# Attention with triangular systems: the diagonal blocks move by copies and 32x32 transposes instead of through DRAM

## The chip, the cores and the metric

The kernel runs on one core of a Trainium2 chip, as one program. The metric is the device time of an execution in microseconds; of several executions the median counts. TensorE is called PE in the profile, VectorE DVE, ScalarE ACT, GpSimd POOL, and SyncE SP; a DMA queue belongs to the engine that issues its transfers (SPq, ACTq).

## The reference, cut to what matters

The program is a transformer of two layers on 2 x 512 tokens of width 256. Each layer is a residual of an attention and of a mixture of experts, each behind a layer norm. The change touches only the attention of layer 0, which has 16 heads of width 16:

```python
s = einsum("bihd,bjhd->bhij", k, k) * scale      # keys with keys, strictly below the diagonal
p = exp(s - max) / sum                           # softmax over j < i
A = p * beta[..., None] + eye(T)                 # unit lower triangular, T = 512
u = solve_triangular(A, v, lower=True)
o = softmax(q k^T * scale, causal) @ u
```

So for each batch and head a triangular system of 512 x 512 is solved, with one right-hand side of 16 columns.

## The kernel before

**Units.** The attention goes through four units (UNITS); a unit is one batch element and eight heads (GH), with four row tiles of 128 tokens each (NI), so 32 tiles "head x row tile". For a unit the kernel computes the row maxima of the scores (row_scores on TensorE, maxima on VectorE), then the transposed scores of keys with keys and their exponentials into E (keys on the partitions, queries along the free axis; exps on ScalarE), sets the upper part to zero with affine_select (select, L853, on POOL) and sums the columns with matmuls (L354). ScalarE copies the sums (L775), TensorE turns them, and VectorE makes from them the factor g = -beta / sum (scale, L591 to L610).

**The inversion.** Each of the 32 diagonal tiles of 128 x 128 has four diagonal blocks of 32 x 32 (SB). All 128 blocks of a unit are inverted at once (invert, L614): a partition holds one block, partition 32 s + e the block s of tile e, in LB, with 32 x 32 numbers along the free axis. To bring the blocks there, SP stores the diagonal tiles of E to DRAM (L893, four transfers) and loads them back rearranged (L899, four). VectorE multiplies them by g (L623), and 31 steps follow (L629 to L648), each with a product (L637) and an addition (L646) for the even and the odd columns: 61 products and 61 additions. The inverse is in Y; L650 makes a copy YT with the two free axes exchanged, in the space of LB. SP stores both to DRAM (L902, L903) and loads them (L909) as XT (four transfers) and XR (three), block-diagonal matrices with rows on the partitions. XT and XR are set to zero by POOL before (L841, L843, and for later units L864, L866).

**The levels and the solve.** With XT and XR TensorE and VectorE join the blocks to inverses of 64 and then of 128 in eight steps (sums, join; scaled_sums L677, joined L663, L666, L660), and solve goes through the four row tiles. Both engines wait ahead of these for XT and XR (L481, L482 and L725, L726).

**Order.** Each engine has its own list of work, written out by hand, and semaphores between them. VectorE's order: maxima of unit 0, scale(0), two calls of rotate_and_split, invert(0), four more such calls; then for each unit the levels, with the maxima of the next unit between them, the solve, scale and invert of the next unit, outputs, and in units 0 and 1 the first eight heads of maxima of the unit after the next (L740 to L742). rotate_and_split (L547) rotates and splits a part of the queries and keys of all units; ScalarE stores its result (store_parts, L248, called at L789) and then goes on to the zero fills of two DRAM buffers (L797, L800). For each unit ScalarE then copies for the solve (L808, L813), takes the exponentials of the next unit's keys, those of this unit's queries (L822), and copies the outputs (copy_outputs, L783), between which it issues loads of the stacks. POOL does the selects: for each unit the next unit's keys, then this unit's queries, eight heads with two instructions each. TensorE applies the queries' exponentials in two halves of four heads (attend, L451) and turns the outputs (L459), which VectorE takes in outputs (L707, L709).

## Time and profile before

| what | value |
|---|---|
| median of three executions | 1398.63 us (1397.51 to 1401.36) |
| span of the profiled execution, first to last instruction | 1391.0 us |
| its own time | not listed apart; the span and the few us around it |
| mean granted clock of TensorE | 0.713 of full speed |
| busy: TensorE, VectorE, ScalarE, POOL | 834.2, 568.9, 219.3, 250.9 us |
| transfers through DRAM for the blocks | 68, on SP's queue |

A timeline row gives the start of an instruction in us from the span's start, its duration in us, the engine, the line of the code, the operation with output and inputs, their shapes and a count; a row with a count over 1 merges instructions that follow each other, and its time is from the first start to the last end. In brackets stands the idle time before it and what ended it. The four inversions lie at 126, 282, 410 and 536 us; the attention ends at about 667 us.

### The profile page before, as it was taken

What the parts mean: (1) busy time and instruction counts of PE and PEld (TensorE: products, weight loads), DVE (VectorE), ACT (ScalarE), POOL (GpSimd) and SP (SyncE); (2) the same over time, 40 slices, a digit from 0 to 9 for tenths busy, and PEclk for the clock granted to TensorE, in tenths of its full rate; (3) what the DMA queues carried; (4) which work ended last, traced back from release to release, by engine and by line L of the source; (5) the groups of instructions that cost most, each with busy time, mean ns of one, the idle gap of its engine ahead of it and who ended that gap; (6) DMA issues with size and microseconds to landing.
All of it is one profiled execution on the core that took longest, in us unless ns stands there. A gap on an engine that the chain in (4) does not pass through costs nothing. (4 is left out here: it accounts for less than half of the span.)

```text
span 1391.0 us, 16655 instructions
## 1 busy us (share of the span) xinstructions
PE 834.2 (60%) x5790; PEld 532.8 (38%) x5791; DVE 568.9 (41%) x1712; ACT 219.3 (16%) x345; POOL 250.9 (18%) x303
## 2 busy tenths in 40 slices
PE   5475477658775865467500387788870435289990
PEld 3232244326432632243400265556650213246660
DVE  5346864188329616320550022222223456223332
ACT  2030000410140033003100122222220112011110
POOL 3010000310040015001067300000007740400004
PEclk9557555765576556557655699999995657589996
DMA  3506710465059103800392377667763310111113
GB/s 129 69 16 131 172 74 2 88 91 145 3 98 179 46 3 76 265 1 0 95 409 106 125 207 208 197 207 211 201 184 92 100 50 0 54 46 45 45 38 98
DMA packets 158348, 149.78 MB, mean 108 GB/s; under 512 B 58576, under 2 KB 144976, under 8 KB 157264
## 3 DMA queue, kind: packets, MB, share of 16 engines
q1 hardware_dynamic: 130608, 85.00, 23.5%
q10 hardware_dynamic: 20000, 43.00, 10.9%
q0 software_dynamic: 7680, 20.98, 4.7%
q8 instruction: 37, 0.61, 0.2%
q14 instruction: 23, 0.19, 0.0%
HBM read 81.89 MB, written 66.85 MB: 107 GB/s over the span
## 5 line engine op out<-in xcount | busy, mean ns | idle before, releaser
L1089 DVE TENSOR_TENSOR hT<-sg,scores 96x256 f32<-96x256 f32 x64 | 26.7, 417 | 250.7 <-ACT sg L1125 250.7
L1000 PE MATMUL misc<-cf,xg 128*128 128x128 f32 x256 | 42.5, 290 | 138.4 <-DMA xg<-expert_rows 138.3
L575 DVE TENSOR_REDUCE nm<-scores 128x1 f32<-128x128 f32 (+3 forms) x256 | 106.2, 482 | 44.9 <-PE scores L318 44.4
L1020 PE MATMUL scores<-xgT,wgu 128*96 128x256 f32 x512 | 121.6, 380 | 0.0
L1202 POOL DMA_INDIRECT gb<-expert_outputs,gather_slots x64 | 66.9, 1046 | 281.2 <-SPq L1195 262.0
L853 POOL TENSOR_SCALAR_AFFINE_SELECT E<-E 128x256 f32<-128x256 f32 x64 | 24.5, 406 | 426.4 <-ACT E L768 426.4
L1000 PEld LDWEIGHTS misc<-cf,xg 128*128 128x128 f32 x256 | 27.7, 143 | 162.6 <-issue 93.9
L1020 PEld LDWEIGHTS scores<-xgT,wgu 128*96 128x96 f32 x512 | 80.4, 164 | 20.8 <-ACT xgT L1117 0.2
L1441 PE MATMUL scores<-w,xgT 128*128 x184 | 87.9, 602 | 0.3 <-issue 0.3
L315 PE MATMUL scores<-stack_B,stack_k 96*128 96x128 bf16 (+3 forms) x128 | 49.9, 468 | 52.2 <-DVE nm L575 24.4
L318 PE MATMUL scores<-cb 128*128 128x128 bf16 x256 | 80.0, 314 | 0.0
L1136 POOL DMA_INDIRECT expert_rows<-xn_moe,scatter_slots x64 | 62.5, 977 | 70.0 <-DVE gather_slots L1066 50.8
L1117 ACT COPY xgT<-misc 128x512 f32<-128x512 f32 x64 | 37.5, 585 | 216.2 <-PE misc L1000 216.1
L1008 PE MATMUL scores<-wd,hT 96*128 96x256 f32 x256 | 65.9, 379 | 0.1
L315 PE MATMUL scores<-stack_B,stack_q 96*128 96x128 bf16 (+3 forms) x128 | 50.2, 468 | 14.1 <-DVE nm L575 14.1
L637 DVE TENSOR_TENSOR tmp<-Y,LB 128x120 f32<-128x120 f32 (+35 forms) x244 | 52.3, 252 | 0.3
L646 DVE TENSOR_TENSOR Y<-Y,tmp 128x120 f32<-128x120 f32 (+35 forms) x244 | 52.2, 251 | 0.1
L1008 PEld LDWEIGHTS scores<-wd,hT 96*128 96x128 f32 x256 | 48.5, 190 | 8.9 <-DVE hT L1089 0.5
L145 PE MATMUL misc<-cf,xn_lin 128*128 128x128 f32 x16 | 3.9, 425 | 79.8 <-DVE xn_lin L128 79.8
L761 ACT COPY mrow<-misc 96x128 bf16<-96x128 bf16 x8 | 2.1, 261 | 309.0 <-PE misc L305 309.0
L1260 DVE SCALAR_TENSOR_TENSOR X<-gb,w,X 128x256 f32<-128x256 f32 x64 | 31.0, 484 | 44.5 <-DMA gb<-expert_outputs,gather_slots 42.8
L1082 DVE COPY yb<-scores 128x512 f32<-128x512 f32 x64 | 44.2, 691 | 5.3 <-PE scores L1008 0.5
(217 smaller groups left out, 1503.5 us busy)
## 6 DMA issues: line engine op xcount, KB each, us to landing
expert_rows<-zero ACTq DMA_DIRECT2D x32, 512.0 KB, 5.6
xg<-expert_rows SPq DMA_DIRECT2D x64, 256.0 KB, 3.5
expert_outputs<-yb SPq DMA_DIRECT2D x64, 256.0 KB, 3.6
wgu<-in_wgu SPq DMA_DIRECT2D x64, 192.0 KB, 2.4
diagonals<-E SPq DMA_DIRECT2D x16, 512.0 KB, 5.8
w<-in_w ACTq DMA_DIRECT2D x8, 1024.0 KB, 16.3
wd<-in_wd SPq DMA_DIRECT2D x64, 96.0 KB, 2.2
w<-in_w ACTq DMA_DIRECT2D x8, 512.0 KB, 18.9
```

Of the source, the lines that this page charges most:

```text
L315: nc.tensor.matmul(scores[:, slot, o:o + w], stk[c][0:KR, u % 2, h, it * P:w], stk["B"][0:KR, u % 2, h, 0:w], start=True, stop=False)
L318: ins = nc.tensor.matmul(scores[:, slot, o + w - P:o + w], identb, mask[c, it], start=False, stop=True)
L575: ins = nc.vector.tensor_reduce(nm[:, c, NI * h + it:NI * h + it + 1], scores[:, slot, o:o + (it + 1) * P], AX.X, ALU.max, negate=True)
L637: nc.vector.tensor_tensor(part, Yc[:, x, 0:n, k:k + 1].to_broadcast([P, n, w]), LB[:, k:k + 1, k + 1:SB].to_broadcast([P, n, w]), ALU.mult ...
L646: nc.vector.tensor_tensor(below, below, part, ALU.add).then_inc(s_inv, 1)
L1000: ins = nc.tensor.transpose(misc[:, j % 2, c:c + P], xg[:, j, t, k * P:(k + 1) * P], identf)
L1008: ins = nc.tensor.matmul(scores[:, j % 2, 512 + t * D:512 + (t + 1) * D], hT[:, j % 2, t * P:(t + 1) * P], wd[:, j, :], start=True, stop=True)
L1020: ins = nc.tensor.matmul(scores[0:F0, j % 2, g * CAP:(g + 1) * CAP], wgu[:, j, k, g * F0:(g + 1) * F0], xgT[:, j % 2, k, :], start=(k == 0 ...
L1082: nc.vector.tensor_copy(yb[:, j].rearrange("p t d -> p (t d)"), scores[:, j % 2, 512:1024]).then_inc(s_yv, 1)
L1136: pool.indirect_dma_start(out=xbuf, out_offset=bass.IndirectOffsetOnAxis(ap=isc[:, t, k:k + 1], axis=0), in_=xn[:, t, :], in_offset=None, ...
L1202: pool.indirect_dma_start(out=gb[:, g % NG, :], out_offset=None, in_=ybuf, in_offset=bass.IndirectOffsetOnAxis(ap=ig[:, t, k:k + 1], axis= ...
L1441: ins = nc.tensor.matmul(scores[:, j, g * F1:(g + 1) * F1], xgT[:, j, k, :], w13[:, bass.ds(e, 1), k, g * F1:(g + 1) * F1].rearrange("p e ...
```

## The change

The blocks no longer go through DRAM. E is copied by 16 instructions of 32 partitions into a new tile, turned (eight on ScalarE in key_softmax, eight on VectorE in gather_blocks, ahead of scale); VectorE's 32x32 transpose brings it into LB, whose two free axes now stand the other way round, so that the multiplication by g and the products of the steps index it accordingly. After the steps a transpose of Y into turned takes L650's place, and ScalarE copies from there into XT (fill_XT, four instructions); three transposes on VectorE write XR. XT and XR are zeroed once only. For the space of the new tile the zero tile has half its width, and the zero fills read it repeatedly. The diff, with little of what surrounds each place:

```diff
@@ -86,7 +86,7 @@
...
         s_out, s_zf = sem("stored"), sem("slots_zeroed")
-        zero = sb("zero", [P, 1024])
+        zero = sb("zero", [P, 512])
         base0 = cf[:, 1161:1225]
@@ -185,7 +185,7 @@
...
             Y = sba("Y", [P, SB, SB])
-            YT = LB
+            turned = sba("turned", [P, SB, SB])
             tmp = sba("tmp", [P, 2, SB * SB // 8 + SB // 4])
@@ -196,9 +196,6 @@
...
             scr = nc.dram_tensor("split_heads", [2, 3, D, N], BF16, kind="Internal").ap()
-            edd = nc.dram_tensor("diagonals", [2, GH * NI, P, P], F32, kind="Internal").ap()
-            xsd = nc.dram_tensor("inverses", [2, 2, P, SB, SB], F32, kind="Internal").ap()
-
             s_pj, s_rf, s_parts = sem("projected"), sem("projection_read"), sem("parts_split")
@@ -210,9 +207,8 @@
...
             s_den, s_ng, s_gt, s_g = sem("denominators"), sem("g_ready"), sem("g_turned"), sem("g_in_blocks")
-            s_ed, s_lb, s_y, s_ys, s_z, s_z2, s_xt, s_xr = (sem("diag_stored"), sem("blocks_loaded"), sem("blocks_inverted"),
-                                                sem("inverses_stored"), sem("XT_zeroed"), sem("XR_zeroed"),
-                                                sem("XT_loaded"), sem("XR_loaded"))
+            s_ga, s_gv, s_y = sem("blocks_gathered_by_scalar"), sem("blocks_gathered_by_vector"), sem("inverses_turned")
+            s_z, s_z2, s_xt, s_xr = sem("XT_zeroed"), sem("XR_zeroed"), sem("XT_filled"), sem("XR_filled")
             s_tt, s_t1, s_pq, s_lv = sem("level_T"), sem("level_T1"), sem("level_PQ"), sem("level_joined")
@@ -244,6 +240,13 @@
...
                 return range(first + max(0, q - 1) * n // 7, first + q * n // 7)
+
+            def diagonal_block(u, s, it):
+
+                rows = slice(SB * s, SB * (s + 1))
+                o = OFF[it] + SB * s
+                return (turned[rows].rearrange("p i (h t) -> p h i t", t=NI)[:, :, :, it],
+                        E[rows, :, o:o + SB])
@@ -478,8 +481,8 @@
...
-                        pe.wait_ge(s_xt, 16 * 4 * (u + 1))
-                        pe.wait_ge(s_xr, 16 * 3 * (u + 1))
+                        pe.wait_ge(s_xt, 4 * (u + 1))
+                        pe.wait_ge(s_xr, 3 * (u + 1))
                         pe.wait_ge(s_fa, 16 * u + 8)
@@ -588,6 +591,18 @@
...
+                    def gather_blocks(u):
+                        dve.wait_ge(s_dk, GH * (u + 1))
+                        if u:
+                            dve.wait_ge(s_xt, 4 * u)
+                        for s in range(2, P // SB):
+                            for it in range(NI):
+                                to, of = diagonal_block(u, s, it)
+                                nc.vector.tensor_copy(to, of).then_inc(s_gv, 1)
+                        dve.wait_ge(s_ga, 8 * (u + 1))
+                        dve.wait_ge(s_gv, 8 * (u + 1))
+                        link(nc.vector.transpose(LB[:].rearrange("p i j -> p (i j)"), turned[:].rearrange("p i e -> p (i e)")))
+
                     def scale(u):
@@ -613,15 +628,12 @@
...
-                        if u:
-                            dve.wait_ge(s_ys, 32 * u)
                         flat = Y[:].rearrange("p c i -> p (c i)")
...
                         nc.vector.memset(flat[:, SB * SB - 1:SB * SB], 1.0)
-                        dve.wait_ge(s_lb, 16 * 4 * (u + 1))
                         link(nc.vector.tensor_tensor(
-                            LB[:], LB[:], G[:].unsqueeze(1).to_broadcast([P, SB, SB]), ALU.mult))
+                            LB[:], LB[:], G[:].unsqueeze(2).to_broadcast([P, SB, SB]), ALU.mult))
@@ -636,7 +648,7 @@
...
                                     part, Yc[:, x, 0:n, k:k + 1].to_broadcast([P, n, w]),
-                                    LB[:, k:k + 1, k + 1:SB].to_broadcast([P, n, w]), ALU.mult).then_inc(s_inv, 1)
+                                    LB[:, k + 1:SB, k:k + 1].rearrange("p i j -> p j i").to_broadcast([P, n, w]), ALU.mult).then_inc(s_inv, 1)
                                 inverted[0] += 1
@@ -647,8 +659,11 @@
...
                         dve.wait_ge(s_inv, inverted[0])
-                        link(nc.vector.tensor_copy(YT[:], Y[:].rearrange("p c i -> p i c")))
-                        nc.vector.sem_inc(s_y, 1)
+                        nc.vector.transpose(turned[:], Y[:].rearrange("p c i -> p i c")).then_inc(s_y, 1)
+                        dve.wait_ge(s_z2, 1)
+                        for s in range(P // SB - 1):
+                            rows, c = slice(SB * s, SB * (s + 1)), SB * (s % 2)
+                            nc.vector.transpose(XR[rows, :, c:c + SB].rearrange("p e c -> p c e"), Y[rows]).then_inc(s_xr, 1)
@@ -713,6 +728,7 @@
...
                         maxima(0, m, m % 2)
+                    gather_blocks(0)
                     scale(0)
@@ -722,8 +738,8 @@
...
                         last = u + 1 == UNITS
-                        dve.wait_ge(s_xt, 16 * 4 * (u + 1))
-                        dve.wait_ge(s_xr, 16 * 3 * (u + 1))
+                        dve.wait_ge(s_xt, 4 * (u + 1))
+                        dve.wait_ge(s_xr, 3 * (u + 1))
                         for q in range(8):
@@ -734,6 +750,7 @@
...
                         if not last:
+                            gather_blocks(u + 1)
                             scale(u + 1)
@@ -771,8 +788,24 @@
...
                             exps(u, 0, h)
+                        act.wait_ge(s_dk, GH * (u + 1))
+                        if u:
+                            act.wait_ge(s_xt, 4 * u)
+                        for s in range(2):
+                            for it in range(NI):
+                                to, of = diagonal_block(u, s, it)
+                                nc.scalar.copy(to, of).then_inc(s_ga, 1)
                         act.wait_ge(s_den, u + 1)
                         nc.scalar.copy(bankT[:], misc[:, 0, :]).then_inc(s_dc, 1)
+
+                    def fill_XT(u):
+                        act.wait_ge(s_y, u + 1)
+                        act.wait_ge(s_z, 1)
+                        if u:
+                            act.wait_ge(s_us, 4 * u)
+                        for s in range(P // SB):
+                            rows = slice(SB * s, SB * (s + 1))
+                            nc.scalar.copy(XT[rows, :, rows], turned[rows].rearrange("p i e -> p e i")).then_inc(s_xt, 1)
@@ -789,16 +822,17 @@
...
                             load_stacks(act, 1)
+                    fill_XT(0)
                     for u in range(UNITS):
...
                                 act.wait_ge(s_ones, 2)
-                                act.wait_ge(s_xt, 16 * 4 * (u + 1))
-                            act.dma_start(xb_z[u * (NZ // UNITS) + z], zero[:]).then_inc(s_zf, 16)
+                            act.dma_start(xb_z[u * (NZ // UNITS) + z].rearrange("p (a n) -> p a n", a=2),
+                                          zero[:].unsqueeze(1).to_broadcast([P, 2, 512])).then_inc(s_zf, 16)
                         for z in range(NZ1 if u + 1 == UNITS else 0):
                             n = min(4, TL - 4 * z)
-                            act.dma_start(xs[4 * z * P:(4 * z + n) * P, :].rearrange("(p n) d -> p (n d)", n=n),
-                                          zero[:, 0:n * D]).then_inc(s_zf1, 16)
+                            act.dma_start(xs[4 * z * P:(4 * z + n) * P, :].rearrange("(p n) d -> p n d", n=n),
+                                          zero[:, 0:D].unsqueeze(1).to_broadcast([P, n, D])).then_inc(s_zf1, 16)
                         if u + 1 < UNITS:
@@ -828,6 +862,8 @@
...
                             load_stack(act, u + 2, "q")
+                        if u + 1 < UNITS:
+                            fill_XT(u + 1)
                     act_transposes(act, 1)
@@ -859,12 +895,6 @@
...
                             select(u + 1, 0)
-                            pool.wait_ge(s_dk, GH * (u + 2))
-                            pool.wait_ge(s_us, 4 * (u + 1))
-                            link(nc.gpsimd.memset(XT[:], 0.0))
-                            nc.gpsimd.sem_inc(s_z, 1)
-                            link(nc.gpsimd.memset(XR[:], 0.0))
-                            nc.gpsimd.sem_inc(s_z2, 1)
                         select(u, 1)
@@ -887,28 +917,6 @@
...
                                              mrow[32 * part:32 * part + 32, c, :]).then_inc(s_ml, 16)
-
-                        sp.wait_ge(s_dk, GH * (u + 1))
-                        for it in range(NI):
-                            sp.dma_start(edd[u % 2].rearrange("(h i) j q -> i j h q", i=NI)[it],
-                                         E[:, :, OFF[it]:OFF[it] + P]).then_inc(s_ed, 16)
-                        sp.wait_ge(s_ed, 16 * 4 * (u + 1))
-                        if u:
-                            sp.wait_ge(s_ys, 32 * u)
-                        for s in range(P // SB):
-                            sp.dma_start(LB[32 * s:32 * s + 32],
-                                         edd[u % 2, :, SB * s:SB * (s + 1), SB * s:SB * (s + 1)]).then_inc(s_lb, 16)
-                        sp.wait_ge(s_y, u + 1)
-                        sp.dma_start(xsd[u % 2, 0], Y[:]).then_inc(s_ys, 16)
-                        sp.dma_start(xsd[u % 2, 1], YT[:]).then_inc(s_ys, 16)
-                        sp.wait_ge(s_ys, 32 * (u + 1))
-                        for x, (dst, zeroed, loaded) in enumerate(((XT, s_z, s_xt), (XR, s_z2, s_xr))):
-                            sp.wait_ge(zeroed, u + 1)
-                            for s in range(P // SB - x):
-                                c = SB * (s % 2 if x else s)
-                                sp.dma_start(dst[SB * s:SB * (s + 1), :, c:c + SB],
-                                             xsd[u % 2, x, 32 * s:32 * s + 32]
-                                             .rearrange("e c i -> c e i")).then_inc(loaded, 16)
```

## Rows read from the trace of the kernel before

**Rows 1.** The page: busy time of each engine, share of the span, instructions.

```profile
PE 834.2 (60%) x5790; PEld 532.8 (38%) x5791; DVE 568.9 (41%) x1712; ACT 219.3 (16%) x345; POOL 250.9 (18%) x303
```

**Rows 2.** Waits of 0 to 700 us: who waited for whom, us in total, times, longest.

```profile
DVE LB L623 <- DMA LB<-diagonals: 16.4, 3, 7.7
```

**Rows 3.** Timeline of VectorE, unit 0: start, us, instruction, idle before and its releaser.

```profile
125.68 1.22 DVE L623 TENSOR_TENSOR LB<-LB,G 128x1024 f32<-128x1024 f32 x1
...
147.33 1.04 DVE L650 COPY LB<-Y 128x1024 f32<-128x1024 f32 x1
...
167.86 0.86 DVE L677 TENSOR_TENSOR early<-scores,ng 32x256 f32<-32x256 f32 x2 [0.25 <-DVE early L560]
```

**Rows 4.** Timeline of VectorE, around the inversions of units 1 and 2.

```profile
270.97 0.19 DVE L595 TENSOR_SCALAR den<-misc 128x32 f32<-128x32 f32 x1 [14.39 <-PE misc L361]
...
273.39 0.91 DVE L619 MEMSET Y<- 128x1024 f32 x1 [0.39 <-DVE G L607]
...
282.22 1.23 DVE L623 TENSOR_TENSOR LB<-LB,G 128x1024 f32<-128x1024 f32 x1 [7.73 <-DMA LB<-diagonals]
...
305.51 1.03 DVE L650 COPY LB<-Y 128x1024 f32<-128x1024 f32 x1
...
410.08 1.23 DVE L623 TENSOR_TENSOR LB<-LB,G 128x1024 f32<-128x1024 f32 x1 [6.11 <-DMA LB<-diagonals]
```

**Rows 5.** Timeline of VectorE, around the inversion of unit 3.

```profile
532.39 0.91 DVE L619 MEMSET Y<- 128x1024 f32 x1 [0.39 <-DVE G L607]
...
536.08 1.22 DVE L623 TENSOR_TENSOR LB<-LB,G 128x1024 f32<-128x1024 f32 x1 [2.59 <-DMA LB<-diagonals]
...
559.99 1.07 DVE L650 COPY LB<-Y 128x1024 f32<-128x1024 f32 x1
...
563.10 0.26 DVE L707 RECIPROCAL rec<-misc 128x16 f32<-128x16 f32 x1 [1.10 <-PE misc L459]
...
574.72 0.86 DVE L677 TENSOR_TENSOR early<-scores,ng 32x256 f32<-32x256 f32 x2 [10.90 <-PE scores L381]
```

**Rows 6.** Timeline of POOL; last, all selects of L853: ns min/median/max, starts.

```profile
262.47 0.76 POOL L853 TENSOR_SCALAR_AFFINE_SELECT E<-E 128x256 f32<-128x256 f32 x2 [0.37 <-ACT E L768]
...
285.62 0.77 POOL L853 TENSOR_SCALAR_AFFINE_SELECT early<-early 128x256 f32<-128x256 f32 x2 [5.98 <-ACT early L768]
...
544.75 11.40 POOL L853 TENSOR_SCALAR_AFFINE_SELECT early<-early 128x256 f32<-128x256 f32 x4 [5.98 <-ACT early L768]
...
L853 POOL TENSOR_SCALAR_AFFINE_SELECT early<-early x32: 401/406/10309, 275.2 to 646.5; 128x256 f32<-128x256 f32 x32
```

**Rows 7.** Lines by form: busy us, mean ns of one, idle before; VectorE, then ScalarE.

```profile
L637 DVE TENSOR_TENSOR tmp<-Y,LB 128x126 f32<-128x126 f32 x20 | 5.1, 286 | 0.0
...
L586 DVE TENSOR_TENSOR nmr<-nm,nms 128x32 f32<-128x32 f32 x8 | 1.5, 192 | 0.3
...
L600 DVE SCALAR_TENSOR_TENSOR ng<-den,VB 128x32 f32<-128x32 f32 x4 | 0.8, 211 | 0.1
...
L1057 DVE TENSOR_TENSOR slot<-slot,cf 128x512 f32<-128x512 f32 x1 | 0.7, 691 | 0.0
...
L1058 DVE TENSOR_SCALAR slot<-slot 128x512 f32<-128x512 f32 x1 | 0.4, 427 | 0.0
...
L1247 ACT ACTIVATE low<-low 128x1024 f32<-128x1024 f32 x4 | 4.2, 1056 | 18.0 <-DVE low L1267 18.0
```

**Rows 8.** Timeline of ScalarE and its DMA issues, units 0 and 3.

```profile
153.18 14.88 ACTq L251 DMA_DIRECT2D split_heads<-early  x4
...
561.76 0.58 ACT L783 COPY bankT<-misc 128x512 f32<-128x512 f32 x1 [12.94 <-PE misc L451]
...
611.44 0.37 ACT L813 COPY bankT<-misc 128x256 f32<-128x256 f32 x1 [49.09 <-PE misc L433]
```

**Rows 9.** Timeline of TensorE before the levels of unit 3.

```profile
557.65 1.07 PE L451 MATMUL misc<-early,U 128*32 128x512 f32 x2 [10.10 <-POOL EQ L853]
...
573.51 1.07 PE L381 MATMUL scores<-XR,E 32*32 32x32 f32 x32 [10.46 <-DMA XR<-inverses]
```

## The prediction

> **What bounds the kernel now.** I began with busy times: no engine is near full, TensorE at 60% and VectorE at 41% of the span [rows 1], so the end is set by chains of waits. The chain view covers only the last part of the program, so for the attention stage I used the waits and then the timelines, engine by engine. The waits name what the change attacks: VectorE idles three times, 16.4 us in all, before L623 for the blocks to come back from DRAM [rows 2]. For units 1 and 2 the second trip through DRAM is hidden: after an inversion VectorE goes on with eight heads of maxima. The timelines then give the order on VectorE, which is almost gapless around an inversion and therefore sets the pace there.
>
> The reader should see this in them. Unit 0: L623 starts at 125.68, the inversion's steps end in the copy L650 at 147.33, four calls of rotate_and_split follow, and L677 starts at 167.86, 0.25 us behind the last of them; the transfers were long in [rows 3]. So in unit 0 nothing waits for DRAM. Units 1 and 2: L623 waits 7.73 and 6.11 us [rows 4]. Unit 3: L623 waits 2.59 us, L677 comes at 574.72 after 10.90 us of waiting for sums [rows 5], and the sums wait 10.46 us for XR [rows 9].
>
> **The change, part by part.** *Gathering.* Eight copies each on ScalarE and VectorE and one transpose. In unit 1 they can start at 263.2, at the end of the last select of the keys [rows 6], and VectorE then idles until 270.97 anyway [rows 4]. Eight copies of 256 elements lie between eight operations of 32 elements and of 512 [rows 7], 1.5 to 5.5 us, nearer 3, and the transpose is some 1.2 (below); ScalarE waits for L354's sums in that time. Cost 0; were the cover gone, 4 to 6 us per unit. ScalarE's denominators copy stands behind its eight copies, but its sums come later.
>
> *The awaited transfer, removed.* Once G is there, L623 can start as soon as Y is set: 0.91 us and a short wait, 1.0 us after L619's start. It comes at 274.39 instead of 282.22 (7.8 us: the wait of 7.73 and 0.1), in unit 2 by 6.2 us earlier (6.11 and 0.1), in unit 3 at 533.39 instead of 536.08 (2.7) [rows 4, 5]. Unit 0 gains 0.
>
> *The steps read LB down a column.* L637 now takes its second input at a step of 32 words instead of 1. The 61 products of an inversion have the sum of (k+1)(31-k), k from 0 to 30, = 5456 elements. What does a far step cost? L600 has a second input at a far step: 211 ns for 32 elements, where L586 with both inputs dense takes 192: 0.59 ns more per element, if its being another form (scalar_tensor_tensor) costs nothing. L650 reads Y at 32 words: on 512 elements a pass of two per step takes 427 ns and of one per step 691, so a step is 1.03 ns and a dense copy of 1024 would be 0.69 us; it takes 1.04 us [rows 3], 0.67 ns more per step [rows 7]. Bounds: 0 (the copy may be slow for another reason, such as its two streams meeting), and 1.04 ns (one more step per element). I take 0.64, between the two rows, since L600 has the same form, a second input beside a first: 3.5 us per inversion. The Trainium skill, SBUF - State Buffer, in the part on Door 1, says that a line of SBUF has 16 bytes and that access by access to a new line pays a penalty, free up to a step of 4 fp32. It names no price for VectorE; by that rule the product steps cannot stay as they are, and both rows above agree.
>
> *The transposes.* No row shows one. Nearest: a 128x1024 operation at one element per step, L623, 1.22 us [rows 3], and as a lower bound two per step, 0.69 us; as an upper one each element twice, 2.3. I take 1.22 with dense reads, as the transposing of words has no second input and nothing promises two per step. The first, Y read at a far step, 1.22 + 0.66 = 1.9 us, takes the place of L650's 1.04: +0.85. The three into XR are new, and I count them, on 32 partitions, like one on 128: 3 x 1.22 = 3.7 us. They write at a far step, for which I find no price and take none; at the price of reads it would be 2 us per inversion. The Trainium skill, VectorE: DVE Perf Modes, "The three transpose paths", gives 311 ns for 128x128 bf16; estimated from there with 896 more elements at 1.03 ns, 1.24 us.
> So one inversion costs VectorE 3.5 + 0.85 + 3.7 = 8.0 us more (0.2 + 3.7 = 3.9 if far steps are free).
>
> *Selects beside the inversion.* From L623 to L650 it was 21.65 us in unit 0, 23.29 in unit 1 (unit 2 is like it) and 23.91 in unit 3 [rows 3 to 5]. Unit 0 has none of POOL's selects beside it, the others 8 to 10 of 16 (they begin with 285.62 and 544.75 [rows 6]): 0.2 us each. Starting earlier, all 16 fall beside: +1.6, +1.6, +1.0.
>
> *XT through ScalarE.* Four copies of 32x1024 elements, read at a far step. The nearest, L1247 with 128x1024 from SBUF, took 1.06 us [rows 7]; with far reads from 1.06 to 1.9, taken as 1.3, nearer to the row since nothing prices ScalarE's far reads: 5.2 us. Queued ahead in unit 0 are store_parts 2 to 7, whose last issue waits for the last rotation (the issues ended at 168.06 [rows 8]); behind it the zero fills and the copy of the maxima, which nobody is near to needing. In the others it stands behind copy_outputs.
>
> *Dropped*: 68 transfers on SP's queue and six POOL memsets. Nobody waited for the memsets, and SP's next work comes far later: 0. The zero fills, cut to 2 and 1 KB pieces, are issued within the 49 us that ScalarE idles before L813 in unit 3 [rows 8]: 0; without that cover, as much as their issue grows, some microseconds.
>
> **The sum, unit by unit.** Unit 0: rotations end at 167.6 + 8.0, last issue +0.5, XT +5.2, sums until L677 +1.2 (574.72 - 573.51 [rows 5, 9]) = 182.5 against 167.86: **+14.6**. What was overlapped now stands in line, since XT waits behind a store that waits behind the whole of VectorE's work. Unit 1: -7.8 + 8.0 + 1.6 = **+1.8**. Unit 2: -6.2 + 8.0 + 1.6 = **+3.4**. XT is hidden in both by the eight heads of maxima. Unit 3: L650's place 559.99 - 2.7 + 1.0 + 3.5 = 561.8, transpose 563.7, XT 568.9, sums 1.2 = 570.1 against 574.72: **-4.6**. Together +15.2 us on a span of 1391.0. The page does not list this execution's own time apart; the median of the three runs is 1398.63, 7.6 us above the span, and I carry those over: **1413.8**.
>
> **The rivals.**
> *Far steps are free* (the side of no loss). Place: the 61 products and the first transpose of each inversion, and ScalarE's four copies. Then an inversion costs 3.9 us more and XT 4.2: unit 0 +9.5, unit 1 7.8 - 3.9 - 1.6 = -2.3, unit 2 -0.7, unit 3 559.99 - 2.7 + 1.0 + 1.2 + 4.2 + 1.2 = 564.9, -9.8. Sum -3.3: 1395.3. Since 18.5 us lie between 0 and 0.64 ns, the sign turns at about 0.1 ns per element. For: L650 is a copy on two streams, L600 another form, so each row has a way out. Against: they come to nearly the same price, 0.59 and 0.67 ns. If transposes also ran two per step (0.69 us), a further 7 us: 1388.
> *Far steps cost a whole step* (1.04 ns): 10.6 us per inversion and 7.6 for XT, unit 0 +19.6, then +4.4, +6.0, +0.4: +30, 1429.
> *POOL is held off.* In unit 3 one select took 10.31 us beside the inversion, from 544.75 to 555.06, TensorE's L451 began only at 557.65, and ScalarE's copy at 561.76 [rows 6, 8, 9]. The fifth head's select came 2 us after the steps' start in unit 1 (285.62), and passed; from now on it comes about 10 us after it in all units, amid the longest steps. Released only at the steps' end (about 301.2 in unit 1), the second L707 would come 2.6 + 5.4 later (555.06 to 557.65, and from there to 563.10 [rows 5]), at 309.2, where VectorE arrives at 307.5: +1.7 in units 1 and 2; in unit 3 XT would be copied from 569.1 and L677 come at 575.5, +5.4. Total +8.8: 1422.6. The Trainium skill, SBUF - State Buffer, "Who interferes with whom", says that a VectorE instruction with two SBUF inputs and a GpSimd one that reads SBUF shut each other out; the row agrees, and by the rule the shift would make it commoner. I count it apart, because in the sum a release as before (17.8 us after the steps' start) delays nobody.
>
> **How the numbers follow.** Forecast 0.50; POOL held off 0.15; a whole step 0.13; far steps free 0.15; free with cheap transposes 0.07. Predicted 1413.8. The range goes from the free case less 2 to about 1427, and leaves out the cheap transposes and most of the dearest case. Within 0.3% (4.2 us, about what a measurement of this kernel can tell from no change) lies the free case for two thirds: same 0.10; the other third and the cheap transposes make faster 0.12; slower 0.78.
>
> **What would show it.** L637 by form: 126 elements at 286 ns now [rows 7], about 365 if right. The transposes' rows: 1.9 and 3 x 1.2 us. ScalarE's four copies after the last store issue, L677 of unit 0 near 182; the idle time before L623 gone; in unit 3 L677 4 to 5 us earlier after the same start. Wrong it would be made by products as short as before, by transposes far from 1.2 us, or by a select over 10 us in units 1 and 2.

## The result and the profile after

The changed kernel took **1429.59 us** (median of four runs, 1425.34 to 1436.91). The kernel before, run beside it, took 1398.07 us (1395.89 to 1401.36). The ratio is 1.0233, with a 95% interval of 1.0208 to 1.0257: slower, by 31.5 us, where +15.2 was forecast. The profiled execution of after took 1436.91 us on a span of 1435.2, the longest of the four.

The page of the kernel after; [rows 1] is its counterpart:

```profile
span 1435.2 us, 16671 instructions
PE 850.8 (59%) x5790; PEld 540.3 (38%) x5791; DVE 626.3 (44%) x1760; ACT 266.5 (19%) x393; POOL 260.7 (18%) x297
```

VectorE is busy for 57 us more and ScalarE for 47 more, on a span that is 44 us longer. Their loads say nothing yet, so I went through the timelines in the order of [rows 3 to 5].

VectorE of the kernel after in unit 0 (start, us, instruction, idle before it and its releaser): the first transpose and the denominators, the end of the inversion, the last rotation, the first work of the solve.

```profile
104.81 1.25 DVE L604 STREAM_TRANSPOSE LB<-turned 128x1024 f32<-128x1024 f32 x1 [1.83 <-ACT turned L797]
109.72 0.19 DVE L610 TENSOR_SCALAR den<-misc 128x32 f32<-128x32 f32 x1 [3.66 <-PE misc L364]
...
150.13 1.91 DVE L662 STREAM_TRANSPOSE turned<-Y 128x1024 f32<-128x1024 f32 x1
151.95 5.69 DVE L666 STREAM_TRANSPOSE XR<-Y 32x1024 f32<-32x1024 f32 x3
...
176.01 0.69 DVE L563 TENSOR_TENSOR early<-early 128x512 bf16<-128x512 f32 x1
186.61 0.86 DVE L692 TENSOR_TENSOR early<-scores,ng 32x256 f32<-32x256 f32 x2 [9.91 <-PE scores L384]
```

ScalarE of the same kernel and unit, ACTq being its DMA issues; the first row is four stores merged:

```profile
162.27 14.89 ACTq L254 DMA_DIRECT2D split_heads<-early  x4
177.59 1.91 ACT L808 COPY XT<-turned 32x1024 f32<-32x1024 f32 x1 [68.70 <-DVEq L565]
...
179.53 1.91 ACT L808 COPY XT<-turned 32x1024 f32<-32x1024 f32 x1
...
181.47 1.91 ACT L808 COPY XT<-turned 32x1024 f32<-32x1024 f32 x1
...
183.40 1.91 ACT L808 COPY XT<-turned 32x1024 f32<-32x1024 f32 x1
```

The inverses were turned at 152.0, yet ScalarE starts on XT at 177.59, behind its last store, and ends at 185.3; the solve starts at 186.61. From the denominators to the solve it is 76.89 us against 57.54, which is from 110.32 in the kernel before (below) to 167.86 [rows 3]: +19.35. The gather is fully hidden: its transpose ends at 106.06, and VectorE then waits 3.66 us for the denominators. ScalarE isn't late for them either: after its eight copies it waits 3.53 us for TensorE's sums (3.4 to 3.7 in the other units).

VectorE after, unit 1, against [rows 4]:

```profile
289.21 1.25 DVE L604 STREAM_TRANSPOSE LB<-turned 128x1024 f32<-128x1024 f32 x1 [1.83 <-ACT turned L797]
294.07 0.19 DVE L610 TENSOR_SCALAR den<-misc 128x32 f32<-128x32 f32 x1 [3.62 <-PE misc L364]
...
297.49 1.22 DVE L635 TENSOR_TENSOR LB<-LB,G 128x1024 f32<-128x1024 f32 x1
...
325.92 1.94 DVE L662 STREAM_TRANSPOSE turned<-Y 128x1024 f32<-128x1024 f32 x1
327.80 5.78 DVE L666 STREAM_TRANSPOSE XR<-Y 32x1024 f32<-32x1024 f32 x3
```

The wait of 7.73 us is gone: L635 starts 3.4 us after the denominators, not 11.25. But its steps last 28.43 us instead of 23.29, and 7.7 us of transposes stand in the place of one copy.

POOL in unit 1, a row that merges four selects:

```profile
308.84 13.50 POOL L889 TENSOR_SCALAR_AFFINE_SELECT early<-early 128x256 f32<-128x256 f32 x4 [5.98 <-ACT early L785]
```

The first of the four is held for 12.30 us by itself, to within 5 us of the steps' end, and likewise the first of four in unit 2 (12.14, from 445.20) and in unit 3 (12.33, from 578.58). In unit 3 this can be seen on ScalarE, whose copy of the outputs waits for TensorE, and TensorE for those selects:

```profile
598.23 0.59 ACT L816 COPY bankT<-misc 128x512 f32<-128x512 f32 x1 [15.58 <-PE misc L454]
...
598.84 1.94 ACT L808 COPY XT<-turned 32x1024 f32<-32x1024 f32 x1
```

VectorE has `turned` done at 597.6, so the hold costs 1.2 us there; ScalarE's four copies then lead to L692:

```profile
607.88 0.42 DVE L692 TENSOR_TENSOR early<-scores,ng 32x256 f32<-32x256 f32 x1 [3.03 <-PE scores L384]
```

The prices, VectorE of the kernel after by form (busy us, mean ns of one, idle before), against [rows 7]:

```profile
L666 DVE STREAM_TRANSPOSE XR<-Y 32x1024 f32<-32x1024 f32 x12 | 22.7, 1892 | 0.3
L662 DVE STREAM_TRANSPOSE turned<-Y 128x1024 f32<-128x1024 f32 x4 | 7.8, 1938 | 0.1
L649 DVE TENSOR_TENSOR tmp<-Y,LB 128x126 f32<-128x126 f32 x20 | 6.8, 374 | 0.0
L604 DVE STREAM_TRANSPOSE LB<-turned 128x1024 f32<-128x1024 f32 x4 | 5.0, 1245 | 7.3 <-ACT turned L797 7.3
```

A product of 126 elements takes 374 ns instead of 286 (365 was forecast). A dense transpose takes 1245 ns, one with far reads 1938, and, unlike what I had taken, one with far writes takes 1892 too.

I call **path stretch** the time from the denominators to the start of the solve (units 0 and 3) or to the first maxima behind the inversion (units 1 and 2). Rows of the kernel before at which they start (units 0, 2 and 3; for unit 1 see [rows 4]), and the end in unit 1:

```profile
110.32 0.19 DVE L595 TENSOR_SCALAR den<-misc 128x32 f32<-128x32 f32 x1 [24.78 <-PE misc L361]
...
308.15 3.26 DVE L575 TENSOR_REDUCE nm<-scores 128x1 f32<-128x128 f32 x8
...
400.46 0.19 DVE L595 TENSOR_SCALAR den<-misc 128x32 f32<-128x32 f32 x1 [15.30 <-PE misc L361]
...
529.98 0.19 DVE L595 TENSOR_SCALAR den<-misc 128x32 f32<-128x32 f32 x1 [15.81 <-PE misc L361]
```

And the end in unit 1 of the kernel after, where the stretch started at 294.07 (above):

```profile
335.07 3.27 DVE L578 TENSOR_REDUCE nm<-scores 128x1 f32<-128x128 f32 x8
```

The stretches in us:

| | unit 0 | unit 1 | unit 2 | unit 3 | sum |
|---|---|---|---|---|---|
| before | 57.54 | 37.18 | 35.63 | 44.74 | 175.1 |
| after | 76.89 | 41.00 | 40.94 | 44.04 | 202.9 |
| measured difference | +19.35 | +3.8 | +5.3 | -0.7 | +27.8 |
| predicted | +14.6 | +1.8 | +3.4 | -4.6 | +15.2 |

The rest of the two profiled spans, 16.4 us, lies outside these stretches; whether the change causes it is the first question below.

### The profile page after: what moved, and what is told of

Its sections match the earlier page's. It is cut to its first block and busy times, and to the rows that moved or that the text cites. A ratio compares the mean times of both kernels' runs of the same rounds, so it can differ in the third digit from the quotient of the medians.

```text
span 1435.2 us, 16671 instructions
## 1 busy us (share of the span) xinstructions
PE 850.8 (59%) x5790; PEld 540.3 (38%) x5791; DVE 626.3 (44%) x1760; ACT 266.5 (19%) x393; POOL 260.7 (18%) x297
## 3 DMA queue, kind: packets, MB, share of 16 engines
q10 hardware_dynamic: 26272, 43.00, 10.7%
## 5 line engine op out<-in xcount | busy, mean ns | idle before, releaser
L889 POOL TENSOR_SCALAR_AFFINE_SELECT E<-E 128x256 f32<-128x256 f32 x64 | 24.6, 407 | 439.0 <-ACT E L785 439.0
L1008 PEld LDWEIGHTS misc<-cf,xg 128*128 128x128 f32 x256 | 27.8, 143 | 164.6 <-issue 94.0
L889 POOL TENSOR_SCALAR_AFFINE_SELECT early<-early 128x256 f32<-128x256 f32 x32 | 49.0, 1556 | 138.6 <-ACT early L785 138.5
L649 DVE TENSOR_TENSOR tmp<-Y,LB 128x120 f32<-128x120 f32 (+35 forms) x244 | 69.9, 327 | 0.3
L454 PE MATMUL misc<-early,U 128*32 128x512 f32 (+3 forms) x128 | 35.6, 737 | 41.9 <-POOL EQ L889 41.9
L284 PE MATMUL scores<-xnT,early 128*128 128x512 f32 x64 | 31.0, 643 | 35.0 <-DVEq L558 34.3
```

The costliest lines, as they stand in the source:

```text
L649: nc.vector.tensor_tensor(part, Yc[:, x, 0:n, k:k + 1].to_broadcast([P, n, w]), LB[:, k + 1:SB, k:k + 1].rearrange("p i j -> p j i").to_br ...
L889: ins = nc.gpsimd.affine_select(out=d, in_=d, pattern=[[0, 2], [1, P]], base=0, channel_multiplier=-1, compare_op=ALU.is_ge if c else ALU. ...
L1008: ins = nc.tensor.transpose(misc[:, j % 2, c:c + P], xg[:, j, t, k * P:(k + 1) * P], identf)
```

## The experiments

**Theory A:** the time goes where VectorE's and ScalarE's new work lies on the path: products at a far step, transposes with far writes, XT copied behind the last store. **Rival B:** POOL's held selects set what follows. **Rival C:** the loss is largely TensorE's clock, in the stretches between. In these runs the kernel before took 1412 to 1414 us (not 1398), so they are compared with a second run of the changed kernel and with the kernel before beside them. Four of them (products dense, XT early, XR by ScalarE, XR twice) ran beside a kernel before of 1412.9 us, while beside that second run it took 1414.1: their differences in time from the changed kernel are good to about 1 us. The path stretches repeat better than that.

### The changed kernel and the kernel before again

> The changed kernel itself once more, beside the kernel before on the chip of this call, as the base for the others. Its path stretches (denominators to the start of the solve in units 0 and 3, to the first maxima in units 1 and 2) should be 76.9, 41.0, 40.9 and 44.0 us again, 27.8 us over those of before in sum; what its time is above or below that is TensorE's clock between the inversions.

> The kernel before itself with its trace, on the chip of this call: here it ran at about 1413 us instead of 1398, while the changed kernel's lead over it shrank from 31 to 22 us. If the clock makes that difference (C), its path stretches are 57.5, 37.2, 35.6 and 44.7 us again and the stretches between them are up to 10 to 15 us longer, at a lower granted clock. If not, one of the four path stretches is longer.

The changed kernel took 1436.2 us against 1414.1 for the kernel before, ratio 1.0164 (1.0131 to 1.0197). Its path stretches were 76.87, 40.97, 40.98 and 44.00, those of before 57.54, 36.67, 36.12 and 45.14: **+27.35** in sum, against 24.6 between the two spans (1437.8 and 1413.2). The path stretches repeat within 0.1 us for the kernel after and 0.5 for the one before; the rest of the attention stage does not. Between and behind them, up to the end of the attention, lay 393.8 us after and 382.1 before in the first pair, 381.3 and 384.1 in this one: +11.7 there, -2.8 here, so the change has no steady effect there. TensorE runs the same 820, 836, 836 and 742 matmuls in these four parts in every case, and where a part is over 1.5 us longer than in another run its mean granted clock is lower (us, and that clock as a share of full speed):

| | units 0 to 1 | 1 to 2 | 2 to 3 | behind 3 | TensorE busy in all four |
|---|---|---|---|---|---|
| first pair, before | 103.1, 0.58 | 92.3, 0.57 | 93.9, 0.55 | 92.8, 0.61 | 278.0 |
| first pair, after | 107.5, 0.51 | 95.4, 0.52 | 92.5, 0.58 | 98.5, 0.55 | 292.9 |
| second pair, before | 105.0, 0.56 | 93.0, 0.57 | 93.5, 0.57 | 92.6, 0.61 | 279.2 |
| second pair, after | 104.8, 0.55 | 92.3, 0.56 | 91.4, 0.58 | 92.8, 0.61 | 277.0 |

So rival C fits 11.7 of the 44.2 us between the two spans of the first pair, and nothing in the second. Why the clock was lower there isn't shown.

The kernel before shows why the whole is longer here. For the kernel before on the second occasion, POOL's gathers of the expert outputs (ns min/median/max, first and last start):

```profile
L1202 POOL DMA_INDIRECT gb<-expert_outputs,gather_slots x64: 1011/1015/1699, 1055.7 to 1139.7; - x64
```

Its last layer's matmuls L1441 begin at 1245.1, 105.4 us after the last gather; on the first occasion these were 1223.8 and 1129.6, 94.2 us. The kernel after has 94.9 and 109.8. So I was wrong to expect the 14 us between the attention stretches: 11 of them lie in a stage that the change does not touch. Why that stage differs was not followed up.

### The products read dense rows

```diff
-  link(transpose(LB[:].rearrange("p i j -> p (i j)"), turned ...))
+  link(transpose(LB[:].rearrange("p j i -> p i j"), turned[:]))
-  ... G[:].unsqueeze(2) ... LB[:, k + 1:SB, k:k + 1].rearrange("p i j -> p j i")
+  ... G[:].unsqueeze(1) ... LB[:, k:k + 1, k + 1:SB]
```

> The changed kernel, but the transpose of the gathered blocks writes at a far step, so that the steps' products read dense rows again. Prices (A): VectorE's steps took 28.4 us with far reads beside POOL's selects and 23.3 without them, 25.05 and 21.65 in unit 0; of that some 3.4 us per unit are the reads. The transpose rises from 1.25 to about 1.9 us, and the 3.6 us that VectorE waits before the denominators in units 0 and 1 hide it. With VectorE setting the pace in units 1 and 2, and ScalarE's copies into XT in units 0 and 3 both starting when the inverses are turned (3.4 us earlier; unit 0 keeps them behind the stores, so nothing there): about -3.4 x 3 = -10 us against the changed kernel, near 1419 us, and products of 128 x 126 back at about 290 ns. If POOL's held selects were the cause (B), the steps would stay near 28 us and the time near 1430. If the clock were the main cause (C), the stretches between the inversions would have to change and not the steps.

(The lines above are shortened.) It took 1422.0 us, ratio 1.0071 (1.0046 to 1.0097): 14.2 less than the changed kernel. VectorE by form, then the steps of unit 0:

```profile
L604 DVE STREAM_TRANSPOSE LB<-turned 128x1024 f32<-128x1024 f32 x4 | 7.9, 1976 | 7.3 <-ACT turned L797 7.3
L649 DVE TENSOR_TENSOR tmp<-Y,LB 128x126 f32<-128x126 f32 x20 | 5.1, 289 | 0.0
```
```profile
127.15 1.22 DVE L635 TENSOR_TENSOR LB<-LB,G 128x1024 f32<-128x1024 f32 x1
...
148.80 1.91 DVE L662 STREAM_TRANSPOSE turned<-Y 128x1024 f32<-128x1024 f32 x1
```

The steps take 21.65 us again, and 24.8 instead of 28.4 in the other units; the path stretches fall by 3.4, 3.6, 3.6 and 3.6. Beside them, the same transpose of 128x1024 went from 1245 to 1976 ns by nothing but its writes at a far step: 0.71 ns per element. I had expected unit 0 to stay as it was. It does not, because the stores ahead of the XT copies wait for VectorE's rotations, and these come 3.4 us earlier. POOL's held select is shorter here too, 8.7 to 8.8 us instead of 12.1 to 12.3, and again ends 4.8 us before the steps do in unit 1: its length follows the steps, not the other way round.

### The steps of the kernel before, down a column

```diff
-  LB[:, k:k + 1, k + 1:SB].to_broadcast([P, n, w])
+  LB[:, k + 1:SB, k:k + 1].rearrange("p i j -> p j i").to_broadcast([P, n, w])
```

> The kernel before, but the steps' products read the blocks down a column instead of along a row, as the changed kernel does (the index is swapped, so another triangle is inverted). By the path (A): 3.4 us more of steps in unit 0 and 3.4 to 5 us in units 1 to 3, all of it on the path: +14 to +18 us against the kernel before, a ratio near 1.011. If the reads are hidden or cost nothing: 1.000.

This kernel inverts another triangle of each block, with the same number of elements. It took 1428.5 us, ratio 1.0101 (1.0065 to 1.0137), +14.4. The steps of unit 0 go from 21.65 to 25.09; the path stretches sum to 189.86 against 175.47. Adding the far reads to the kernel before and taking them from the kernel after thus give the same price, some 3.5 us per unit.

### XT ahead of the last stores

```diff
                         if w == 3:
                             load_stacks(act, 1)
-                    fill_XT(0)
+                            fill_XT(0)
```
(The call moves from behind the last stores to ahead of them.)

> The changed kernel, but unit 0's copies of the turned inverses into XT stand on ScalarE ahead of the last stores of the projections instead of behind them. Prices (A): the four copies (7.7 us) ran at 177.6 to 185.3 us, behind a store issue that ended at 177.2; VectorE had nothing to do for 9.9 us before its first work of the solve at 186.6. With the copies done by about 161 us, that work starts when VectorE is through with its rotation, near 177: -8 to -10 us, near 1420.5 us. Rival: the score matmuls or the loads behind the later stores take the place of the copies, and the start moves by under 3 us (1427 to 1430).

It took 1427.4 us, ratio 1.0109 (1.0073 to 1.0145): 8.8 less. ScalarE, then VectorE:

```profile
152.73 7.83 ACT L808 COPY XT<-turned 32x1024 f32<-32x1024 f32 x4 [43.19 <-DVE turned L662]
163.02 14.89 ACTq L254 DMA_DIRECT2D split_heads<-early  x4
```
```profile
177.71 0.42 DVE L692 TENSOR_TENSOR early<-scores,ng 32x256 f32<-32x256 f32 x1 [0.25 <-DVE early L563]
```

The solve now follows the rotations by 0.25 us, as in the kernel before. Unit 0's stretch is 67.34, 9.5 less, and the others are as they were.

### The XR blocks by ScalarE, and the XR blocks twice

```diff
-  for s in range(3): VectorE transposes Y[rows] into XR[rows, :, c:c + SB]
+  nc.vector.transpose(LB, Y)                    # once, dense
+  for s in range(3): ScalarE copies LB[rows] into XR[rows, :, c:c + SB], behind XT
```

> The changed kernel, but the three transposes into XR (1.89 us each on VectorE) are replaced by one dense transpose on VectorE (1.25 us) and three copies on ScalarE (about 1.9 us each) behind those into XT. VectorE is relieved of 4.4 us per inversion, ScalarE gets 5.7 more. By the path as the trace shows it (A): units 1 and 2, where VectorE sets the pace, gain 4.4 each; units 0 and 3, where the first work of the solve waits for ScalarE's copies, lose 5.7 each: +2.6 in all, near 1432 us. If VectorE's work set the pace everywhere, it would be -17 (1412); if ScalarE's did, +23 (1452).

```diff
   for s in range(3):
+      link(nc.vector.transpose(to, Y[rows]))       (to: the same place in XR)
       nc.vector.transpose(to, Y[rows]).then_inc(s_xr, 1)
```

> The changed kernel, but each of the three transposes into XR is made twice: 5.7 us more on VectorE per inversion. By the path (A): unit 0 hides them in the 9.9 us that VectorE waits for the copies into XT; units 1 and 2 pay 5.7 each; unit 3 pays between 0 and 5.7, since the output work of unit 2 stands behind them on VectorE: +11 to +17, near 1443 us. If VectorE's transposes are hidden beside POOL, ScalarE or TensorE (so that the clock or the held selects made the loss), it stays near 1430.

(The lines of both are shortened.) By ScalarE: 1440.5 us (1435.7 to 1448.2), ratio 1.0183 (1.0146 to 1.0221). The path stretches changed by +1.0, -4.7, -4.4 and +5.9, -2.2 in sum, while the time rose by 4.3; the stretches between them were 6.4 us longer, so the time alone would not tell this from no change, and only the stretches do. Unit 0 lost 1.0 us and not the 5.7 expected: ScalarE's copies take longer, but VectorE's rotations, behind which they stand, now end earlier. In unit 3 VectorE waits for ScalarE's seven copies:

```profile
611.32 0.42 DVE L690 TENSOR_TENSOR early<-scores,ng 32x256 f32<-32x256 f32 x1 [13.61 <-PE scores L384]
```

Twice: 1460.9 us, ratio 1.0346 (1.0313 to 1.0379), 24.7 more, where 11 to 17 was expected. The path stretches grew by 5.5, 5.8, 5.9 and 4.3. VectorE's wait before the solve of unit 0 stays what it was, but moves:

```profile
194.09 0.42 DVE L694 TENSOR_TENSOR early<-scores,ng 32x256 f32<-32x256 f32 x1 [9.91 <-PE scores L384]
```

That wait of 9.91 us hid nothing: it is the length of what follows the rotations (store, copies, sums), so whatever makes the rotations late delays it whole. The prediction had this chain right; my expectation for this run had forgotten it.

### Without the queries' selects

```diff
-                        select(u, 1)
+                        for h in range(GH):
+                            pool.wait_ge(s_fa, use(1, u) + h + 1)
+                            nc.gpsimd.sem_inc(s_dq, 1)
```

> The changed kernel without POOL's 16 selects per unit of the queries' exponentials (the causal mask of the query scores is left out; the rest stands). One select of each of units 0 to 2 is held for about 13.5 us while VectorE's steps run. If the held selects set what follows (B), the stretches of units 1 and 2 shrink by some 8.8 us each and the time falls to about 1410. By the path (A) they only take VectorE's time beside them: the steps of units 1 to 3 last 28.4 us against 25.05 in unit 0, where no select of a query runs, and that may fall to 25.05; so 3.4 us in each of units 1 to 3 and near -10 us at the very most, and about 1 us more in unit 3, where ScalarE's outputs wait for the last selects.

This kernel leaves out the causal mask of the queries' scores. It took 1425.7 us, ratio 1.0097 (1.0066 to 1.0128): 10.5 less. VectorE, unit 1, start and end of the steps:

```profile
292.17 1.22 DVE L635 TENSOR_TENSOR LB<-LB,G 128x1024 f32<-128x1024 f32 x1
...
317.40 1.91 DVE L662 STREAM_TRANSPOSE turned<-Y 128x1024 f32<-128x1024 f32 x1
```

The steps last 25.2 us in units 1 to 3, as in unit 0, and the path stretches fall by 0, 3.2, 3.2 and 4.3. So all of B in units 1 and 2 is the time that 16 selects take from VectorE's steps (0.2 us each), which is in the sum of A. Only unit 3 pays 1.1 us for the hold itself.

### All of it together

> The changed kernel with three edits at once: the transpose of the gathered blocks writes at a far step and the products read dense rows; unit 0's copies by ScalarE stand ahead of the last stores; the three transposes into XR are one dense transpose on VectorE and three copies on ScalarE. From the stretches measured for each edit alone: unit 0 76.9 - 3.4 - 9.6 - 4.4 = 59.5 us against 57.5 before, unit 1 41.0 - 3.6 - 4.7 = 32.7 against 37.2, unit 2 40.9 - 3.6 - 4.4 = 32.9 against 35.6, unit 3 44.0 - 3.6 + 5.9 = 46.3 against 44.7: -3.6 us against the kernel before, a ratio near 0.997. If the edits share what they save, it stays above 1.005.

> As the kernel with three edits, but in unit 3 the XR blocks are turned by VectorE as in the change, since there ScalarE's copies stand on the path and VectorE has room. Unit 3 gets back the 5.9 us that it lost (44.0 - 3.6 = 40.4 us against 44.7 before); the others stay at 59.5, 32.7 and 32.9. Sum against the kernel before: +2.0 - 4.5 - 2.7 - 4.3 = -9.5 us, a ratio near 0.993 (0.990 to 0.995). If ScalarE's seven copies were not what unit 3 waited for, it stays at 0.996.

With the three edits: 1408.65 us, ratio **0.9961** (0.9937 to 0.9986). The path stretches were 58.86, 32.66, 32.67 and 46.35, within 0.7 us of the expectation. In units 1 to 3 that is, to 0.3 us, the plain sum of the single edits. In unit 0 it isn't: there XR by ScalarE alone cost 1.0 us, which would give 65.0. Once XT no longer stands behind the stores, VectorE's relief of 4.4 us counts in unit 0 as well. The second kernel differs by one condition:

```diff
+  if u + 1 < UNITS:
       transpose(LB[:], Y[:]); XR by three ScalarE copies
+  else:
+      XR by three VectorE transposes, as in the change
```

It took **1403.2 us against 1412.3, ratio 0.9944 (0.9922 to 0.9965)**, so it is 0.6% faster than the kernel before. Unit 3 on VectorE:

```profile
555.18 1.96 DVE L663 STREAM_TRANSPOSE turned<-Y 128x1024 f32<-128x1024 f32 x1
557.06 6.12 DVE L670 STREAM_TRANSPOSE XR<-Y 32x1024 f32<-32x1024 f32 x3
...
567.51 0.42 DVE L696 TENSOR_TENSOR early<-scores,ng 32x256 f32<-32x256 f32 x1 [2.77 <-PE scores L384]
```

L696 comes 12.33 us after the first of these transposes, as L692 comes 12.2 us behind L662 in the kernel after: ScalarE's copies into XT still set this part. Unit 3's stretch is 40.56, 4.6 us under that of the kernel before beside it; all four sum to 164.75 against 175.47.

| run | path stretches against the kernel after (e6 and e9: against before) | measured time |
|---|---|---|
| products dense | -14.2 | -14.2 |
| XT early | -9.6 | -8.8 |
| XR by ScalarE | -2.2 | +4.3 |
| XR twice | +21.5 | +24.7 |
| no query selects | -10.6 | -10.5 |
| three edits | -4.9 | -5.5 |
| XR split | -10.7 | -9.1 |

## Why the prediction was wrong

The direction was right, and so was the mechanism: which work stands on the path in which unit. Two terms of the sum were too small, and each lies on the path in several units: with a hold that the sum left out they are 12.1 of the 16.3 us by which 31.5 exceeds 15.2. They bring the forecast to 1425.9 us, and the whole of the path stretches to 1426.4, still just inside the range up to about 1427. That the measured time lies beyond it is due to some 3.7 us of the difference between the medians that lie outside the path stretches, which the second comparison (22.1 us in all) doesn't show again.

- **Gathering at cost 0:** right. VectorE idles 3.5 to 3.8 us behind it in each unit, ScalarE 3.4 to 3.7.
- **The awaited transfer:** right. L635 stands 3.4 us behind the denominators in every unit but unit 0.
- **Products down a column, 3.5 us per inversion:** right, though it was worked out from two rows that each had another way out. Unit 0 showed 3.4, and taking them out, or adding them to the kernel before, changed the steps by 3.4 to 3.6.
- **The first transpose, 1.9 us:** right (1.94).
- **The three into XR, "3 x 1.22 = 3.7 us":** the step that failed. "They write at a far step, for which I find no price and take none" set to zero an unknown whose nearest row was the price of far reads. The three took 5.7 us, and the same transpose written densely and at a far step took 1245 and 1976 ns. I had named those 2 us per inversion, but put them neither into the sum nor into the range. They come to +2 in each of units 0, 1 and 2. The Trainium skill, SBUF — State Buffer, in the part on Door 1, speaks of accesses to a new line, not of reads alone. It names no price, but read so it gives these writes a cost above zero, and the runs agree, with 0.71 ns per element for writes and 0.68 for reads (1976 and 1938 against 1245 ns).
- **XT through ScalarE, "taken as 1.3":** the second. A copy took 1.91 us, the upper end I had named, not the nearest row. Four make 7.7 us instead of 5.2: +2.5 in units 0 and 3.
- **Selects, +1.6, +1.6, +1.0:** right. With all 16 beside the steps these take 28.4 us, without them 25.2.
- **POOL held off:** it happened in all of units 1 to 3, which the forecast gave 0.15, but its price was not the 8.8 us of the rival. The sum had the select released 17.8 us after the steps' start, the rival only at their end; it was released 22.4 us after the start, some 5 us before the end. The run without selects gives no cost of the hold in units 1 and 2 and 1.1 us in unit 3. The Trainium skill, SBUF — State Buffer, "Who interferes with whom", calls the pair of ports that VectorE and GpSimd share an exclusive lock, and says, of VectorE's two-port modes, that whoever issues first has it for the whole instruction. The trace agrees in so far as the select was shut out and the steps are 3.2 us shorter without the selects; but it was shut out for 12.30 us, through 54 of VectorE's instructions, so by this trace it is not the one instruction in progress that it waits for.

Unit by unit: unit 0 is +2.0 and +2.5 of a gap of 4.75, units 1 and 2 are +2 each (1.9 to 2.0), unit 3 is +2.5 and 1.1 of 3.9. That is 12.1 of the 12.6 us between 15.2 and 27.8. The medians differ by 31.5 us in the first comparison and by 22.1 in the second, on either side of the 27.8; the part outside the path stretches, +16.4 and -2.8 us in the profiled spans, has no steady sign. In the first pair 11.7 of it goes with a lower granted clock (the table above); what makes the rest, and the lower clock, was not settled. "Far steps cost a whole step" (1429) gave nearly the measured time, and for another reason: the products' price was 3.44 us on 5456 elements, 0.63 ns and not 1.04.

The idea of the change was sound, and its cost lay in where the new work was put. Its products could have kept their dense rows by having the transpose write them so, in time that is idle (the transpose then ends at about 290.5 + 0.7, still 2.9 us ahead of the denominators in unit 1). XT stood behind a queue of stores for which nobody needed it to wait. And units 1 and 2 are paced by VectorE, so work there belongs on ScalarE, while in unit 3 both share it.

## What to carry to other kernels

When two passes through DRAM are replaced by work on the engines, first ask which engine paces each stage, and which queue the new work stands in: here one call moved ahead of four stores was worth 9 us, and moving three blocks from VectorE to ScalarE saved 4.4 to 4.7 us in each of two units and cost 1.0 and 5.9 in the others. An idle time that is the tail of a chain starting at that engine is no cover; doubling the work before it shows which it is. A step with an unknown price on the path goes into the sum at the nearest known price, not at zero.

## What the runs showed of the hardware

- Far steps (32 words of fp32) cost VectorE about as much in writes as in reads: a transpose of 128x1024 took 1245 ns dense (1204 from Y into LB, in the run with XR by ScalarE), 1938 with far reads and 1976 with far writes. On 32 partitions instead of 128, with far writes, it took 1892. ScalarE's copies of 32x1024, all with far reads, took 1.91 us into XT and 1.91 into XR.
- A single POOL select, 0.4 us by itself, was held for some 12 us while VectorE ran its steps back to back, once in each of units 1 to 3, always the first of the second eight, which began 11.3 us after L635. The first eight, beside the first and short steps, took 0.4 to 0.7 us each. In the kernel before the same select passed in 0.41 us in unit 1, 3.4 us after L623, and was held for 10.31 us in unit 3, 8.7 us after it. The 16 cost VectorE's steps 3.2 us together.
- Two occasions of the same kernel before differed by 14 us (1%), 11 of it in one stage of the last part; a comparison across the occasions would have hidden some of the single edits.
